# First-step states and row maxima turned on VectorE, with DMAs and GpSimd, instead of TensorE transposes

## The reference

```
# attention 0: 16 heads of 8; q and k are unit vectors per head
state = q
for _ in range(2):
    sim = einsum('bqhd,bkhd->bqhk', state, k)
    state = einsum('bqhk,bkhd->bqhd', softmax(sim), v)
x = x + residual + state.reshape(B, S, H) @ Wo + bo

# attention 1: heads of 8 in a reshaped layout, scores masked by blocks
scores = where(mask, q @ k.T / sqrt(8), -1e9)
out = softmax(scores) @ v
```

## Time and profile before

| what | value |
|---|---|
| median of 3 runs | 3903.79 us (3903.47 to 3909.41) |
| the profiled execution | 3903.75 us |
| its span, first to last instruction | 3902.0 us |
| mean granted clock of TensorE | 0.911 of full speed |
| busy: TensorE, VectorE, ScalarE, GpSimd | 86%, 61%, 55%, 27% |
| Exp on ScalarE (L712) | 1536 times, 1025 ns each |
| reduction on VectorE (L875) | 1024 times, 1223 ns each |

### The profile page before, as it was taken

The page is one execution under the profiler, slowest core; times in us unless marked ns, Lnnn a source line. Parts: engine busy times, 40 slices in busy tenths (PEclk is TensorE's granted clock), DMA queues, the critical chain, the costliest instruction groups (busy, mean ns, idle before and its releaser), DMA issues. The chain is left out here.

```text
span 3902.0 us, 54943 instructions
## 1 busy us (share of the span) xinstructions
PE 3366.3 (86%) x20118; PEld 1699.3 (44%) x20118; DVE 2383.3 (61%) x5217; ACT 2158.5 (55%) x2817; POOL 1063.0 (27%) x2225
## 2 busy tenths in 40 slices
PE   4778888898989989898998989898998989898886
PEld 2224343344444434444444445444453444444553
DVE  2335575666757666675757666675766667575563
ACT  1444566565555656555566656556665655564432
POOL 3122213141412323141332414132231414121311
PEclk6678799898989989898999989899998989899997
DMA  1000000000000000000001000000000000000100
GB/s 37 0 1 28 4 28 4 28 28 31 28 31 25 7 28 29 31 28 31 25 7 45 12 31 29 31 27 24 34 4 31 28 31 28 28 25 11 48 28 30
DMA packets 71257, 95.81 MB, mean 25 GB/s; under 512 B 40304, under 2 KB 58160, under 8 KB 70864
## 3 DMA queue, kind: packets, MB, share of 16 engines
q1 hardware_dynamic: 70992, 92.29, 7.2%
HBM read 82.76 MB, written 4.78 MB: 22 GB/s over the span
## 5 line engine op out<-in xcount | busy, mean ns | idle before, releaser
L712 ACT ACTIVATE probs<-ps 128x1024 f32<-128x1024 f32 x1536 | 1574.8, 1025 | 1006.0 <-PE ps L576 970.3
L875 DVE TENSOR_REDUCE negmax<-ps 128x2 f32<-128x1024 f32 x1024 | 1251.8, 1223 | 723.2 <-PE ps L617 713.7
L576 PE MATMUL ps<-qT,kT 32*128 32x512 f32 x3072 | 826.0, 533 | 374.0 <-ACT probs L712 354.8
L593 PE MATMUL ps<-probs,v 128*32 128x512 f32 x6144 | 907.2, 666 | 0.1
L576 PEld LDWEIGHTS ps<-qT,kT 32*128 32x128 f32 x3072 | 305.5, 195 | 1083.8 <-ACT probs L712 733.4
L1083 POOL TENSOR_TENSOR xe<-xT_m,G 128x512 f32<-128x512 f32 x288 | 368.7, 1283 | 1135.9 <-PE ps L654 910.3
L654 PE MATMUL ps<-xe,w_sb 128*128 128x256 f32 x2304 | 650.9, 408 | 12.1 <-POOL xe L1083 8.3
L617 PE MATMUL ps<-kT,qT 32*128 32x512 f32 x2048 | 555.2, 537 | 73.1 <-DVE negmax L875 73.0
L654 PEld LDWEIGHTS ps<-xe,w_sb 128*128 128x128 f32 x2304 | 404.9, 195 | 249.0 <-issue 177.4
L742 ACT ACTIVATE th<-ps 128x256 f32<-128x256 f32 x576 | 221.9, 385 | 335.1 <-PE ps L654 333.6
L940 DVE SCALAR_TENSOR_TENSOR th<-th,ps 128x256 f32<-128x256 f32 x576 | 238.8, 415 | 254.7 <-ACT th L742 242.3
(11 more groups left out here) (168 smaller groups left out, 2773.2 us busy)
## 6 DMA issues: line engine op xcount, KB each, us to landing
G<-gates_dram SPq DMA_DIRECT2D x96, 768.0 KB, 6.2
v<-v_tok SPq DMA_DIRECT2D x256, 18.0 KB, 1.9
X<-in_x SPq DMA_DIRECT2D x16, 256.0 KB, 8.1
out<-X SPq DMA_DIRECT2D x16, 256.0 KB, 2.3
w_sb<-in_w SPq DMA_DIRECT2D x1, 1152.0 KB, 5.5
w_sb<-in_w SPq DMA_DIRECT2D x1, 576.0 KB, 6.3
gates_dram<-gT SPq DMA_DIRECT2D x32, 18.0 KB
wqkv<-in_wqkv SPq DMA_DIRECT2D x2, 192.0 KB, 2.4
```

What stands on the lines that cost most here:

```text
L576: nc.tensor.matmul(ps[:, B_ST + h, :], kT[a][rows, g * S + kc * P:g * S + (kc + 1) * P], qT[a][rows, g * S:(g + 1) * S], start=True, stop= ...
L593: ins = nc.tensor.matmul(ps[ROWS * j:ROWS * (j + 1), B_UT, :], v[:, at:at + ROWS], probs[:, n % QUADS, j, :], start=(kc == 0), stop=(kc == ...
L712: nc.scalar.activation(probs[:, quad % QUADS, j:j + 2, :], ps[:, B_ST:B_ST + 2, :], ACT.Exp).then_inc(sem["exp_done"], 1)
L875: nc.vector.tensor_reduce(negmax[job_no(kind, b, g) % 2][:, tc, 2 * half:2 * half + 2], ps[:, B_SM:B_SM + 2, :], AX_X, ALU.max, negate=Tru ...
```

## The change

In S1 windows ScalarE's copy and both sets of TensorE transposes go. VectorE turns the bank `B_UT` in 32x32 blocks into `uts` (`uts_state`), which puts each head's queries on that head's 32 partitions; it divides there, fills `qstack` (a doubled rounded copy and the remainder) and turns `qstack` in 32x32 blocks back into `uts` (`state`). GpSimd copies `uts` to `qT` and raises `state_done`, on which the first `sm` of S2 and the next writers of `uts` wait.

In max jobs the negative maxima of a job lie in a 128x32 tile `negmax` (16 of the 32 columns used). VectorE turns it in 32x32 blocks to `negmaxT`; four DMAs on SP, one per band of 32 partitions, move its 16 rows to the four rows 24, 56, 88 and 120 of `maxrow` (128x512, zero elsewhere); GpSimd adds `maxrow` to `qT`. As only row 24 of a head carries the maximum now, `key_rows` makes that row one for every key in L1. `turn`, `state` and `rows` are taken from the list of events that need a side bank (`turn` stays in it for S2 and L1), and the lags follow the engines.

```diff
@@ -51,16 +51,16 @@
 S2_MAX_AT = (31, 42, 63, 73)
 L1_AT = (16, 32, 56, 72)
 L1_MAX_AT = (0, 10, 21, 52)
-SIDE_EVENTS = frozenset("ffn_xt ffn_y p0_xt p0_qkv p0_op turn state rows o_t o_y m_xt m_logits m_gt m_gu m_down "
+SIDE_EVENTS = frozenset("ffn_xt ffn_y p0_xt p0_qkv p0_op turn o_t o_y m_xt m_logits m_gt m_gu m_down "
                         "p1_xt p1_qkv p1_op".split())
 
 HOP = 0.8
 LAG = {
-    "act": {n: HOP for n in "st ffn_xt p0_xt p1_xt o_t m_xt p0_op p1_op state m_gt m_gu".split()},
-    "dve": {**{n: HOP for n in "sm ffn_y p0_qkv p1_qkv turn rows o_y m_logits m_down m_probs".split()},
+    "act": {n: HOP for n in "st ffn_xt p0_xt p1_xt o_t m_xt p0_op p1_op m_gt m_gu".split()},
+    "dve": {**{n: HOP for n in "sm ffn_y p0_qkv p1_qkv turn o_y m_logits m_down m_probs".split()},
             "m_gu": 2 * HOP},
-    "pool": {**{n: HOP for n in "ffn_stats p0_stats p1_stats m_stats p0_sums p0_hi p1_hi m_index".split()},
-             "turn": 2 * HOP},
+    "pool": {**{n: HOP for n in "ffn_stats p0_stats p1_stats m_stats p0_sums p0_hi p1_hi m_index state".split()},
+             "rows": 2 * HOP},
     "sp": {"m_gt": 2 * HOP, "p1_values": HOP},
     "pe": {},
 }
@@ -122,9 +122,10 @@
     for kc in range(TC):
         t.at(start + 2 * kc + 3.3, "pv", kind, b, g, kc)
     t.at(start + 10.2, "uts", kind, b, g)
-    t.at(start + 11.2, "turn", kind, b, g)
     if kind == "S1":
-        t.at(start + 14.2, "state", b, g)
+        t.at(start + 11.2, "state", b, g)
+    else:
+        t.at(start + 11.2, "turn", kind, b, g)
 
 
 def max_job(t, start, kind, b, g):
@@ -263,8 +264,10 @@
         qk = [sb(f"qk{i}", [P, TC, 2 * P]) for i in range(2)]
         probs = sb("probs", [P, QUADS, NG, S])
         uts = sb("uts", [P, S])
-        mx = sb("mx", [P, TC * NG, ROWS])
-        negmax = [sb(f"negmax{i}", [P, TC, NG]) for i in range(2)]
+        s1t = uts[:].rearrange("p (x e) -> p x e", e=ROWS)
+        negmax = [sb(f"negmax{i}", [P, ROWS]) for i in range(2)]
+        maxrow = sb("maxrow", [P, S])
+        negmaxT = sb("negmaxT", [P, ROWS])
         rden = sb("rden", [P, TC * NG])
         st8 = sb("st8", [P, TC * NG, HD])
         stats = sb("stats", [P, TC, 6])
...
@@ -400,8 +403,8 @@
         side_read = [ctx.enter_context(nc.semaphore(f"side_read{i}")) for i in range(SIDES)]
         gates_in = [ctx.enter_context(nc.semaphore(f"gates_in{i}")) for i in range(3)]
         sem = signals(nc, ctx, "dve_step pool_step "
-                               "st_ready exp_done pv_done ut_copied sm_ready sm_read mx_ready rows_added "
-                               "state_hi state_lo o0_part o1_part o_added "
+                               "st_ready exp_done pv_done ut_copied sm_ready sm_read mx_ready "
+                               "state_turned state_done rows_in rows_added o0_part o1_part o_added "
                                "ffn_var ffn_r ffn_biased ffn_done "
                                "p0_var p0_r p0_res p0_squared p0_summed p0_unit p0_hi p0_lo "
                                "p1_var p1_r p1_res p1_hi p1_lo v_moved "
@@ -436,6 +439,10 @@
 
         def job_no(kind, b, g):
             return no[("mx", kind, b, g)]
+
+        def states_up_to(n):
+
+            return sum(1 for key, w in no.items() if key[0] == "uts" and key[1] == "S1" and w < n)
 
         def run_no(b, k):
             return no[("m_stats", b, k)]
@@ -483,6 +490,16 @@
                     cols = slice(c * 3 * S, (c + 1) * 3 * S)
                     sp.dma_start(G[:, cols], gates_dram[n % 2][cols].partition_broadcast(P)).then_inc(gates_in[c], 16)
 
+            def rows(n, kind, b, g):
+
+                target = maxrow[ADD0::ROWS, :].rearrange("j (t b q) -> j b t q", t=TC, b=NG)
+                sp.wait_ge(sem["mx_ready"], n + 1)
+                if n:
+                    sp.wait_ge(sem["rows_added"], n)
+                for i in range(NG):
+                    sp.dma_start(target[:, i],
+                                 negmaxT[ROWS * i:ROWS * i + NG * TC, :]).then_inc(sem["rows_in"], 16)
+
             def p1_values(n, b):
                 sp.wait_ge(*read(("p1_qkv", b, TC - 1)))
                 v = v_sb[1][b % 2][:, 0:TC * NH * VW].rearrange("p (k g x) -> p k g x", k=TC, g=NG)
...
@@ -595,17 +612,13 @@
                 ins.then_inc(sem["pv_done"], 1)
 
             def turn(n, kind, b, g):
-                pe.wait_ge(sem["ut_copied"], n + 1)
+                pe.wait_ge(sem["ut_copied"], window_no(kind, b, g) + 1)
                 turn_chunks(("turn", kind, b, g), [uts[:, tc * P:(tc + 1) * P] for tc in range(TC)])
-
-            def state(n, b, g):
-                pe.wait_ge(sem["state_lo"], n + 1)
-                turn_chunks(("state", b, g), [qstack[:, NG * tc:NG * (tc + 1), :] for tc in range(TC)])
 
             def sm(n, kind, b, g, half, tc):
                 a = layer(kind)
                 if n % (2 * TC) == 0 and a == 0:
-                    pe.wait_ge(*read(("state", b, g)))
+                    pe.wait_ge(sem["state_done"], no[("state", b, g)] + 1)
                 elif n % (2 * TC) == 0:
                     pe.wait_ge(*read(("p1_op", b, TC - 1, 0)))
                     pe.wait_ge(*read(("p1_op", b, TC - 1, 1)))
@@ -617,10 +630,6 @@
                     nc.tensor.matmul(ps[:, B_SM + h, :], qT[a][rows, g * S + tc * P:g * S + (tc + 1) * P],
                                      kT[a][rows, g * S:(g + 1) * S], start=True, stop=True).then_inc(sem["sm_ready"], 1)
 
-            def rows(n, kind, b, g):
-                pe.wait_ge(sem["mx_ready"], n + 1)
-                turn_chunks(("rows", kind, b, g), [mx[:, NG * tc:NG * (tc + 1), :] for tc in range(TC)])
-
             def o_t(n, b, a):
                 pe.wait_ge(o_part[a], NG * (b + 1))
                 turn_chunks(("o_t", b, a), [O[a][:, tc, :] for tc in range(TC)])
...
@@ -713,15 +721,15 @@
                                      ACT.Exp).then_inc(sem["exp_done"], 1)
 
             def uts_copy(n, kind, b, g):
+                if kind == "S1":
+                    return
+                act.wait_ge(sem["state_done"], states_up_to(n))
                 act.wait_ge(sem["pv_done"], TC * (n + 1))
                 dst, source = uts[:], ps[:, B_UT, :]
                 if kind == "L1":
                     dst = dst.rearrange("p (t c) -> p c t", c=NH)
                     source = source.rearrange("p (c t) -> p c t", c=NH)
                 nc.scalar.activation(dst, source, ACT.Copy).then_inc(sem["ut_copied"], 1)
-
-            def state(n, b, g):
-                copy_out(("state", b, g), qT[0][:, g * S:(g + 1) * S])
 
             def m_probs(n, b, k):
                 act.wait_ge(sem["m_shifted"], n + 1)
...
@@ -850,17 +858,35 @@
                     dve.wait_ge(*read(("p1_qkv", b, TC - 1)))
                 nc.vector.tensor_copy(heads1(i)[:, :, :, 0:HD].bitcast(F32R), source_of(1, i)).then_inc(sem["p1_hi"], 1)
 
+            def uts_state(n, kind, b, g):
+
+                if kind != "S1":
+                    return
+                if no[("state", b, g)]:
+                    dve.wait_ge(sem["state_done"], no[("state", b, g)])
+                dve.wait_ge(sem["pv_done"], TC * (n + 1))
+                nc.vector.transpose(uts[:],
+                                    ps[:, B_UT, :]).then_inc(sem["ut_copied"], 1)
+                dve.wait_ge(sem["ut_copied"], n + 1)
+                link(nc.vector.reciprocal(rden[:], s1t[:, :, HD]))
+                link(nc.vector.tensor_tensor(st8[:], s1t[:, :, 0:HD],
+                                             rden[:].unsqueeze(2).to_broadcast([P, TC * NG, HD]), ALU.mult))
+
+            def state(n, b, g):
+
+                twice = qstack[:, :, 0:2 * HD].rearrange("p x (r d) -> p x r d", r=2).bitcast(F32R)
+                link(nc.vector.tensor_copy(twice, st8[:].unsqueeze(2).to_broadcast([P, TC * NG, 2, HD])))
+                link(nc.vector.tensor_tensor(qstack[:, :, 2 * HD:3 * HD].bitcast(F32R), st8[:], qstack[:, :, 0:HD],
+                                             ALU.subtract))
+                nc.vector.transpose(uts[:],
+                                    qstack[:].rearrange("p x e -> p (x e)")).then_inc(sem["state_turned"], 1)
+
             def turn(n, kind, b, g):
                 key = ("turn", kind, b, g)
                 bank = side_bank(key).rearrange("p (x e) -> p x e", e=ROWS)
                 dve.wait_ge(*filled(key))
                 link(nc.vector.reciprocal(rden[:], bank[:, :, HD]))
                 inv = rden[:].unsqueeze(2).to_broadcast([P, TC * NG, HD])
-                if kind == "S1":
-                    nc.vector.tensor_tensor(st8[:], bank[:, :, 0:HD], inv, ALU.mult).then_inc(read_signal(key), 1)
-                    dve.wait_ge(*read(key))
-                    nc.vector.tensor_copy(qstack[:, :, 0:HD].bitcast(F32R), st8[:]).then_inc(sem["state_hi"], 1)
-                    return
                 a = layer(kind)
                 heads = O[a][:].rearrange("p c (h d) -> p c h d", d=HD)
```

(39 more changed lines are left out.)

13 lines of the change are left out of this document (6 added, 7 removed).

## The result

The changed kernel took 3923.94 us (median of five, 3911.36 to 3925.23), against 3903.79 for the kernel before: ratio 1.0034, 95% interval 1.0020 to 1.0048. It is 0.34% slower, where 1.8% faster was forecast. The profiled execution took 3911.36 us; the other four had granted clocks of 0.879 to 0.882.

The account below looks back on a forecast made before the run. TensorE's queued work was taken to bound most units, ScalarE's Exp or VectorE's maxima others. Per turn -7.7 + 0.5 - 0.3 + 3.0 = -4.5 us, over 16 turns -72, last turn +3: 3903.75 - 69 = 3835 us; range 3775 to 3908.

Parts of the forecast that it names:

- VectorE, +0.5 us a turn: VectorE's queue: new S1 steps add 1.5 us of TensorE wait, removed qT additions save some 1 us.
- Of the four S1 windows one meets a busy loop: S1 windows on VectorE: only one delays a reduction, by 0.7 us; the other three find VectorE waiting or sm a unit away.
- TensorE, -7.7 us: TensorE: 16 transpose groups a turn go, ten at 0.5 us, two at half clock 2.1 us together, the rest little or nothing.
- ScalarE, -0.3 us a turn: ScalarE: S1's uts and state copies go; nearly all lay in idle time, so -0.3 us a turn.
- The clock, +3.0 us a turn: TensorE's clock: without the transposes two low stretches grow together and four units lengthen, +3 us a turn.
- one joined stretch: TensorE's clock: low stretches of 10.1 and 16.9 us join over the 6.9 us between, some 34 us a turn.
- The maxima's path: Transpose, four SP DMAs, GpSimd addition: hidden with 3.4 us of cover at S2, g=3; 3 us once in the last turn.
- Rival 4: Maxima's path late: at 3 us a turn beyond cover, 3883 us; chance 0.18 together with rival 2.
- rival 3: TensorE's clock: other stretches drop to half clock; a loss from 25 us more a turn, 3931 us at 30; chance 0.13.
- Rival 2: ScalarE's and VectorE's loops take TensorE's gain: -0.3 us a turn, 3899 us; chance 0.18 together with rival 4.
- Rival 1: TensorE's clock: transposes don't hold it, so it isn't hurt; -7.5 us a turn, 3787 us; chance 0.15.
- the two signs by which the prediction was to be wrong: VectorE's block transpose twice as dear as the 0.69 us taken, or the low-clock stretch more than doubled.

Follow-up runs that it names:

- e9: Kernel before plus the maxima's half only, with idle transposes in TensorE's waits for Exp and ahead of sm at five units: 3781.59 us, ratio 0.9653.
- e10: Kernel before plus idle transposes in TensorE's waits for Exp and ahead of sm at five units, no other change: 3823.70 us, ratio 0.9773.
- e5: Kernel before plus only S1's half of the change, maxima on their old path: 3955.70 us, ratio 1.0113.
- e6: Kernel before plus only the maxima's half of the change, S1 as before: 3887.41 us, ratio 0.9934.
- e7: e2 with both VectorE transposes of S1 cut from 512 to 32 columns and a maximum for the reciprocal (different result): 3732.51 us, ratio 0.9541.
- e1: Changed kernel with idle, unread transposes at the places of the removed ones: 3937.37 us, ratio 1.0073.
- e2: Changed kernel with groups of four idle transposes in units where TensorE waits for Exp, 17 a steady turn: 3801.52 us, ratio 0.9735.
- e4: e2 with idle 32-row matmuls instead of the idle transposes: 3873.00 us, ratio 0.9895.
- e13: e4 with its idle matmuls on all 128 rows: 3791.62 us, ratio 0.9690.
- e15: Kernel before plus the idle groups of e14 at the same places: 3775.24 us, ratio 0.9631.
- e14: Changed kernel with more idle transposes than e2, only where TensorE waits for Exp, none ahead of sm: 3740.22 us, ratio 0.9541.
- e12: e6 with the four DMAs of the maxima cut into eight: 3889.91 us, ratio 0.9934.
- the clean pair: e14 and e15, changed kernel and kernel before with the same idle groups, none ahead of sm: 3740.22 and 3775.24 us.
- e3: Kernel before plus idle transposes in units where TensorE waits for Exp, as in e2: 3809.26 us, ratio 0.9732.

## Why the prediction was wrong, by its own steps

**How the terms are read.** With the clock held a steady turn gained 2.6 us; the forecast without its clock term was -7.7 + 0.5 - 0.3 = -7.5. The split of the 2.6 is read from the units: -6.2 shortened, +3.6 lengthened. Of the latter 0.8 us stand in units 33, 63 and 65, which lengthen in e9 against e10 too, beside units that lost a group of the maxima; they are counted with TensorE's term. That leaves -5.4 and +2.8.

**VectorE, +0.5 us a turn. This is the step whose mechanism failed.** Durations and busy time were right: 0.712 us for 0.69, 149.4 us of busy time in a turn against 148.4. Its place was not. "Of the four S1 windows one meets a busy loop" counted only the reduction next in the queue. The delay is handed on from one reduction to the next through the steps between, and met loops at units 19 to 23, 37, 53 and 55. It measured +2.8 us a turn, inside the ends of -2 and +6 given for it, and off by 2.3 x 16 = 37 us. That it comes from S1's steps on VectorE is shown twice: e5 has all of the new waits and e6 none, and e7, with 4.3 us a turn less of their time, gives back 2.65 us. That the removed `qT` additions would shorten such waits by 1 us a turn is not borne out: e6, where they are gone, has 183.5 us for 186.4, 0.2 us a turn.

**TensorE, -7.7 us, and ScalarE, -0.3 us a turn. A term too large.** Measured: -5.4 us for both, inside the ends, off by 2.6 x 16 = 42 us. The price of 0.5 us a group was right where TensorE binds the unit: -0.51 to -0.66 at 21, 35, 51, 54 and 84, which lost one group each. But fewer units paid it: unit 11 lost two groups and 0.65 us, 14 and 32 lost 0.39, and 38, 42 and 74 lost 0, 0.06 and 0.17, as the shortened units met a loop's floor. And the forecast paid two groups at half clock at 1.05 us, which a held clock does not.

**The clock, +3.0 us a turn, 48 us in all.** Measured: +20 us of medians less the -35 us with the clock held is 55 us; by the profiled executions (+7.6 us) 43 us. The size was right, and the reading that transposes help to hold the level is shown by e1, e2, e4 and e13. But it was right by luck, for its place was wrong. The forecast took all turns for steady ones. The steady turns got 8 us more at half clock, as read, but it cost them little. In the profiled executions of e15 and e14, the stretches up to the end of turn 2, of turns 3 to 14 and of the rest are 616.6, 2612.2 and 548.8 us, then 604.9, 2587.3 and 549.8: 12 us less, 25 less and 1 more. Without the idle groups the same stretches were 11 us more, 15 less and 11 more. The differences, 23, 10 and 10 us, are what the clock took: 0.8 us of a steady turn and not 3, and three quarters of the whole in the first three and last three turns. Nor was it one joined stretch: it is new ones at units 37 and 53, where S1's half makes `sm` wait. The mean price of a microsecond at half clock is about 0.27 us (e2 to e14: 61 us for 0.030 of clock in some 3770 us, so 230 us of half-clock time).

**The maxima's path, nothing, 3 us in the last turn.** Cover 3.7 us for 3.4, and the last two turns of e14 and e15 are equal within 0.3 us. Rival 4 is dead (e12).

**The sum.** -69 + 37 + 42 - 3 + 7 (55 for 48) = +14 us, with +20 measured. The 6 us left over are nearly those by which 16 x -2.6 = -42 us differs from the -35 of the clean pair: one turn's rows do not hold for all 16. The range ended at 3908 us, since rival 3 alone (0.13) was thought to lie beyond, and no case was given in which VectorE's loss and the clock's meet. Rival 2, whose sign was waits before `sm` well above 186 us (252 measured), named the mechanism, and 2.5 us for the 2.8; its 3899 us leave out the last turn's +3. Rival 3's threshold, 25 us more of each turn at half clock, was not reached (13 us as a mean): by these terms the clock alone would not have made the kernel slower. Rival 1 is refuted by e2 against e4. Neither of the two signs by which the prediction was to be wrong came: the transpose was not dearer, and the low time of a steady turn went from 25 to 33 us. They watched prices, while the faults lay in a queue's order and in turns that were taken for steady ones.

What stays open: which of the 17 idle groups matter was not tried; nor was S1's transpose behind the reduction in VectorE's order, nor the maxima's half with the groups of e14, the fair partner for S1's half.

## What to carry to other kernels

When work moves to an engine that has room on average, follow its queue for several instructions past the new one: a delay is passed on through every instruction between, until the engine idles. When full-array work is taken off TensorE, count what keeps its clock in the stretches that remain, above all in the ramp at the start and the end, where little else does; freed time that ends in a wait is worth nothing, and a few idle full-array matmuls in such waits were worth 3% here. Test two effects that oppose each other with the one held still, and make the held version fair to both kernels: here the groups that held the clock cost 0.5 to 0.9 us in five units of every kernel without S1's new queue, enough to turn the sign of a comparison.

## What the hardware showed that was not expected

The product `st` (L872 now) took 291 ns at best and 1381 at most, mean 447; in the kernel before, reading its operand from the PSUM bank, it took 291 to 293 ns in all 64 cases, but there no GpSimd instruction ran beside any of them. Fifteen of the 64 are long, each beside GpSimd's addition L1009. From the changed kernel's timeline:
```profile
1795.59 1.27 POOL L1009 TENSOR_TENSOR X<-X,bffn 128x512 f32<-128x512 f32 x1
...
1796.15 0.85 DVE L872 TENSOR_TENSOR st<-uts,rden 128x128 f32<-128x128 f32 x1
...
1816.34 0.29 DVE L872 TENSOR_TENSOR st<-uts,rden 128x128 f32<-128x128 f32 x1
```
The first begins during the addition and ends at 1797.00, 0.14 us after it; the second has no GpSimd work beside it. Both operands lie in SBUF since the change. The Trainium skill, page "SBUF — State Buffer", section "SBUF: two separate sides", says that a VectorE operation with two SBUF inputs and a GpSimd operation that reads SBUF exclude one another for the whole instruction, and with that the trace agrees: all 15 end 0.15 us after the addition, wherever in it they began. Whether an operand in PSUM would have spared it, no run here shows. It cost no unit that the unit lengths show (unit 11 shortened by 0.65 us all the same).

Idle full-array work, 272 ns a transpose at full clock and never read, shortened the kernel before by 2.7% (e3) to 3.7% (e15).
